# Running the scores two steps ahead in a fused ViT layer, with the side work placed anew

## The chip, the cores and the metric

The kernel runs on one core of a Trainium2 chip. The metric is the device time of one execution in microseconds (us); the median of three runs of the kernel before is 2177.81 us (2173.88 to 2178.31).

## The reference

The kernel computes one layer of a vision transformer tower for 64 images of 3x224x224 (float32):

```python
h = patches(x) @ W.T + b                       # 196 tokens of 768 -> 192
qkv = layernorm(h, g, b) @ qkv_w.T + qkv_b     # 12 heads of 16
attn = q @ k.T * 16 ** -0.5                    # 196 x 196
attn = attn - 0.2 * (3x3 neighbours of attn, the centre left out)
h = h + softmax(attn) @ v
# expert layer: router (192 -> 192 -> 8), the best 2 of 8 experts, each 192 -> 768 -> 192
h = h + sum_e w_e * (relu(layernorm(h) @ W1_e.T + b1_e) @ W2_e.T + b2_e)
```

## The kernel before

There are two phases. The attention phase (here changed) takes some 1230 us and the expert phase the rest; the second starts when the first has stored all rows and is not touched.

The attention phase works on 32 pairs of images. A pair has six **steps**: three groups of four heads for the first image, then for the second. Each engine runs its own in-order program, and what is in the loop body is written out by hand as a software pipeline: at step `kk` an engine works on parts of several steps and pairs. `Step(body, kk, ahead)` is the step that lies `ahead` steps further, `Pair(body, kk, ahead)` the pair that lies `ahead` pairs further, and `k = kk % 6` is the step within the pair, called step 0 to step 5 below. A loop body has two pairs; in its second the kernel also prepares a part of the experts' weights ("pack").

In each step:

- TensorE computes `scores` of four heads (L607, s_bank, two banks that alternate by head), of the step **one** ahead. VectorE takes their row maxima (`row_maxima`, L824) and splits them into two float16 parts (`split_maxima`, L832, L835).
- TensorE transposes these parts (`transpose_max`, L647) and ScalarE copies them into eight extra rows of q_stack (`copy_max_rows`, L1037), so that `scores_less_max` (L623, t_bank, again two banks) gives the scores, transposed and with the maximum taken off, in one matmul. This is for the same step that the maxima came from, so all of it lies between a step's scores and the next step's `scores_less_max`.
- ScalarE takes the exponentials (L1020), TensorE multiplies by v (`mix`, L636) for the step before, ScalarE copies this out (L1027), TensorE transposes it back (L589), and VectorE divides by the sums (`normalise`, L847, L851) for two steps before.

The neighbour sum is folded into q and k: `beside` (GpSimd, L1201) and `tilde` (VectorE, L912) add a token's neighbours. Plain and tilde forms are split into float16 high (ScalarE, L1073, L1082) and low parts (VectorE, L921, L931), stored to memory by two DMAs (`store_parts`) and read back by six (`stack`, L384), which lay three 32-row blocks for q and three for k over all 12 heads into q_stack and k_stack (double buffered by pair). The first scores of a pair wait for all six.

The **side work**, spread over a pair's six steps, prepares later pairs: cast and split of the patches for pair +2 (`high_patches`, ScalarE L1001; `split_patches`, GpSimd L1193), their projection (`project_patches`, four blocks of 18 matmuls, L519 to L521), `take_h`, layer norm statistics and layer norm (GpSimd), transposition, `project_qk`, `take_qk`, `project_v`, `take_v`. The second layer norm ("_n") of finished pairs runs in step 1 to 4 of the pair after: `sum_rows`, `statistics_n`, `inverse_deviation_n`, `layernorm_n`, `high_rows`, `low_rows`. All DMAs of this phase are issued in order by SyncE's queue, which waits at each for its own condition. Its program at step 3 of the first body also blanks some memory (`blank_memory`).

## Time and profile before

| | |
|---|---|
| median of three runs | 2177.81 us |
| the profiled execution: time, span | 2189.16 us, 2187.4 us |
| TensorE busy (share of the span) | 1891.2 us (86%) |
| VectorE busy | 1461.1 us (67%) |
| ScalarE busy | 1266.8 us (58%) |
| GpSimd busy | 1152.0 us (53%) |
| attention phase: last transposition of attention output ends at | some 1222 us |
| mean granted TensorE clock | 0.925 of full speed |

The busy times overlap, since the engines run beside each other. A matmul's recorded length includes its way through the array, so that TensorE can start another before it ends. The clock is a share of 2.4 GHz; 0.50 is 1.2 GHz. Engine names in rows: PE is TensorE, PEld its weight loads, DVE VectorE, ACT ScalarE, POOL GpSimd, SP SyncE (SPq its queue of DMAs).

### The profile page before, as it was taken

Reading aid. Unit: us, or ns where it says so; the run is one execution under the profiler, and the core shown is the slowest. Engines: PE = TensorE matmul, PEld = TensorE weight load, DVE = VectorE, ACT = ScalarE, POOL = GpSimd, SP = SyncE. Lnnn points to the kernel's source line nnn. Section 1 sums busy time; section 2 is a strip of 40 time slices with the busy share of each in tenths; the row PEclk is TensorE's granted clock in tenths of the full one; section 3 lists DMA queues with packets and bytes.
Section 4 is the critical chain, followed back from the end, with each engine's and each line's share of the span. In section 5 each row is a group of like instructions: output and inputs, shape, how many; then the busy total and the mean of one; then the engine's idle time right before and its main releaser. Section 6 shows DMA issues by size and latency. Waiting matters only on the chain. (4 is left out here: it accounts for less than half of the span.)

```text
span 2187.4 us, 54001 instructions
## 1 busy us (share of the span) xinstructions
PE 1891.2 (86%) x17949; PEld 1406.2 (64%) x17949; DVE 1461.1 (67%) x4652; ACT 1266.8 (58%) x2469; POOL 1152.0 (53%) x1069
## 2 busy tenths in 40 slices
PE   4758888888888989898888479999999999999991
PEld 3546666666666666666665256777777777777771
DVE  4658888888888888888887345655555555554440
ACT  3557788787878788787877323433434343333330
POOL 3335555555555545555552254666666666654452
PEclk7878999999999999999999559999999999999996
DMA  4564746666574747575664237787877878798876
GB/s 142 144 187 143 202 147 190 168 182 168 173 197 146 215 142 198 161 195 157 183 173 132 65 106 197 186 211 184 206 185 205 190 201 194 190 195 184 180 176 193
DMA packets 356572, 382.56 MB, mean 175 GB/s; under 512 B 138388, under 2 KB 319952, under 8 KB 352144
## 3 DMA queue, kind: packets, MB, share of 16 engines
q1 hardware_dynamic: 314768, 338.64, 55.3%
q0 software_dynamic: 41664, 42.12, 11.1%
q8 instruction: 80, 1.31, 0.2%
q14 instruction: 60, 0.49, 0.1%
HBM read 232.83 MB, written 135.46 MB: 168 GB/s over the span
## 5 line engine op out<-in xcount | busy, mean ns | idle before, releaser
L1838 ACT ACTIVATE mh<-mid_bank 128x512 bf16<-128x512 f32 x336 | 200.8, 598 | 464.0 <-PE mid_bank L1529 349.6
L824 DVE TENSOR_REDUCE row_max<-s_bank 98x2 f32<-98x392 f32 x768 | 396.6, 558 | 97.6 <-PE s_bank L607 94.7
L1750 DVE SCALAR_TENSOR_TENSOR ml<-mid_bank,mh 128x512 bf16<-128x512 f32 x336 | 231.6, 689 | 341.9 <-ACT mh L1838 333.7
L1020 ACT ACTIVATE probs<-t_bank 98x392 f32<-98x392 f32 x768 | 340.6, 498 | 42.1 <-PE t_bank L623 31.1
L1904 POOL DMA_INDIRECT sums<-y_out,tail x168 | 265.1, 1578 | 172.9 <-DVE y_out L1780 95.8
L1543 PE MATMUL y_bank<-wst,mh 128*128 128x192 bf16 x1344 | 330.0, 246 | 8.3 <-DVE y_out L1780 7.5
L1546 PE MATMUL y_bank<-wst,ml 128*128 128x192 bf16 x1344 | 330.1, 246 | 0.0
L1545 PE MATMUL y_bank<-wst,mh 128*128 128x192 bf16 x1344 | 329.8, 245 | 0.0
L623 PE MATMUL t_bank<-q_stack,k_stack 104*98 104x196 f16 x1536 | 248.6, 269 | 40.0 <-ACT probs L1020 25.5
L1193 POOL TENSOR_TENSOR x_lo<-x_buf,x_hi 128x588 f16<-128x588 f32 x128 | 188.7, 1478 | 170.6 <-ACT x_hi L1001 112.8
L1889 POOL DMA_INDIRECT slots<-row_r,spot x196 | 190.7, 973 | 98.0 <-issue 56.7
L623 PEld LDWEIGHTS t_bank<-q_stack,k_stack 104*98 104x98 f16 x1536 | 152.5, 130 | 112.3 <-ACT probs L1020 108.6
L519 PE MATMUL p_bank<-wtok_h,x_hi 128*98 128x192 f16 x768 | 201.7, 263 | 18.2 <-POOL x_lo L1193 18.2
L607 PE MATMUL s_bank<-k_stack,q_stack 96*98 96x196 f16 x1536 | 204.0, 256 | 6.1 <-DVE row_max L824 5.3
L520 PE MATMUL p_bank<-wtok_l,x_hi 128*98 128x192 f16 x768 | 199.7, 260 | 0.0
L521 PE MATMUL p_bank<-wtok_h,x_lo 128*98 128x192 f16 x768 | 198.7, 259 | 0.0
L1037 ACT COPY q_stack<-m_bank 8x784 f16<-8x784 f16 x192 | 154.4, 804 | 66.5 <-PE m_bank L647 63.5
L636 PE MATMUL o_bank<-probs,v_buf 98*32 98x196 f32 x3072 | 171.5, 341 | 18.1 <-ACT probs L1020 18.0
L1201 POOL TENSOR_TENSOR beside<-padded 128x1176 f32<-128x1176 f32 x32 | 68.7, 2146 | 195.3 <-ACT padded L1064 195.3
L607 PEld LDWEIGHTS s_bank<-k_stack,q_stack 96*98 96x98 f16 x1536 | 153.2, 130 | 12.7 <-DVE row_max L824 7.4
L1543 PEld LDWEIGHTS y_bank<-wst,mh 128*128 128x128 bf16 x1344 | 134.3, 100 | 41.1 <-issue 19.5
L1545 PEld LDWEIGHTS y_bank<-wst,mh 128*128 128x128 bf16 x1344 | 131.0, 97 | 19.6
(236 smaller groups left out, 4515.7 us busy)
## 6 DMA issues: line engine op xcount, KB each, us to landing
wst<-packed SPq DMA_DIRECT2D x56, 1584.0 KB
x_buf<-in_x_t SPq DMA_DIRECT2D x32, 1176.0 KB, 9.0
q_stack<-stack_parts SPq DMA_DIRECT2D x96, 294.0 KB, 4.8
k_stack<-stack_parts SPq DMA_DIRECT2D x96, 294.0 KB, 6.7
stack_parts<-qk_hi SPq DMA_DIRECT2D x32, 588.0 KB, 2.9
stack_parts<-qk_lo SPq DMA_DIRECT2D x32, 588.0 KB, 2.8
sums<-h_buf SPq DMA_DIRECT2D x32, 294.0 KB
h_in<-sums SPq DMA_DIRECT2D x32, 294.0 KB
```

The costliest lines, as they stand in the source:

```text
L519: nc.tensor.matmul(out, x_hi[:, f, tokens], wtok_h[:, f, :], start=(f == 0), stop=False)
L520: nc.tensor.matmul(out, x_hi[:, f, tokens], wtok_l[:, f, :], start=False, stop=False)
L607: last = nc.tensor.matmul(s_bank[hh % 2][0:HALF, u, 0:TOKENS], q_stack[st.q][0:PARTS, head, head_cols(st, u)], k_stack[st.q][0:PARTS, head ...
L623: last = nc.tensor.matmul(out, k_stack[st.q][:, head, head_cols(st, v)], q_stack[st.q][:, head, head_cols(st)], start=True, stop=True)
L824: nc.vector.reduce_max(row_max[st.odd][:, :, hh:hh + 1], s_bank[hh % 2][0:HALF, :, 0:TOKENS], AX.X).then_inc(max_ready, 1)
L1020: nc.scalar.activation(probs[st.odd][:, hh], t_bank[hh % 2][0:HALF, :, 0:TOKENS], ACT.Exp).then_inc(probs_ready, 1)
L1543: nc.tensor.matmul(o, mh[n % MID][:, cols], high, start=(c == 0 and j % 2 == 0), stop=False, skip_group_check=True)
L1545: nc.tensor.matmul(o, mh[n % MID][:, cols], low, start=False, stop=False, skip_group_check=True)
L1546: last = nc.tensor.matmul(o, ml[n % MID][:, cols], high, start=False, stop=False, skip_group_check=True)
L1750: nc.vector.scalar_tensor_tensor(ml[n % MID][:], mid_bank[n % MID_PS][:], 0.0, mh[n % MID][:], ALU.max, ALU.subtract).then_inc(ml_ready, 1)
L1838: nc.scalar.activation(mh[n % MID][:], mid_bank[n % MID_PS][:], ACT.Relu).then_inc(mh_ready, 1)
L1904: nc.gpsimd.indirect_dma_start(out=total_rows, out_offset=bass.IndirectOffsetOnAxis(ap=to, axis=0), in_=y_out[q][:, j, :], in_offset=None, ...
```

## The change

- The scores are computed two steps ahead (`LOOK`), with their maxima and the split of these. `transpose_max` and `copy_max_rows` stay one step ahead, so the split that they use is made a step earlier.
- The stacks are read back by group of heads, 18 DMAs for a pair in place of six, and the scores of a group wait for its own six. The stores and the first two groups move to step 2 (the low store and what follows it), the third to step 3.
- Patches: loads, casts and splits run three pairs ahead (casts in steps 2 to 5, splits in 3, 4, 5 and 0); the projection, still two pairs ahead, runs in steps 0, 1 and 2 in place of 1 and 2. TensorE's side work is divided between a place among the heads (`between_heads`, before the last two heads' `scores_less_max`) and one at the end.
- VectorE: both `take_h` and the statistics are in step 2; `statistics_n` alone in step 3; both `take_v` in step 4; `normalise` comes after the work between the maxima. GpSimd: the layer norm in step 3, `sum_rows` waits for the plain low part, the second layer norm's work is in step 4.
- ScalarE: `layernorm_n` is divided between steps 0 and 1 of the pair after next, `high_rows` is in step 3, `take_high_tilde` is among the exponentials, and `take_qk` comes after `copy_max_rows`.
- The fill interleaves pairs 0 and 1 and loads pair 2; the pipeline begins at step -4 and drains for 12 steps in place of 7.

```diff
 BODY_PAIRS = 2
 BODY_STEPS = BODY_PAIRS * STEPS
 BODIES = PAIRS // BODY_PAIRS
-DRAIN = STEPS + 1
+DRAIN = 2 * STEPS
+LOOK = 2
+FILL = 4

...
@@ -136,13 +138,16 @@
-    step(0, -1)
+    for kk in range(-FILL, 0):
+        step(0, kk)
     for body in range(2):
         for kk in range(BODY_STEPS):
             step(body, kk)
-    with eng.Fori(2, BODIES - 1) as body:
+    with eng.Fori(2, BODIES - 2) as body:
         for kk in range(BODY_STEPS):
             step(body, kk)
+    for kk in range(BODY_STEPS):
+        step(BODIES - 2, kk)
     for kk in range(BODY_STEPS + DRAIN):
         step(BODIES - 1, kk)
...
@@ -374,15 +386,15 @@
-            def stack(pr, low):
                     sp.wait_ge(parts_stored[low], 16 * (pr.u + 1))
                     for which, r in (((0, 0), (0, 2), (1, 0), (1, 1)), ((0, 1), (1, 2)))[low]:
...
+                        sp.dma_start((q_stack, k_stack)[which][pr.q][32 * r:32 * r + 32, HG * g:HG * (g + 1)],
+                                     src[:, :, g]).then_inc((q_stacked, k_stacked)[which][g], 16)

             def rows(dram, pr):
                 return dram[bass.ds(pr.u, 1)].rearrange("o c p e -> p (o c) e")
@@ -456,35 +468,44 @@
                     for low in range(2):
...
+                    for g in range(GROUPS):
+                        for low in range(2):
+                            stack(Pair(0, 0, 0), low, g)
                     store_h(Pair(0, 0, 1))
+                elif kk < 0:
+                    return
                 elif k == 0:
-                    load_x(Pair(body, kk, 2))
+                    load_x(Pair(body, kk, 3))
                     load_h(Pair(body, kk, -1))
-                    store_rows(Pair(body, kk, -2))
                 elif k == 1:
                     if kk == 1 and not (isinstance(body, int) and body == 0):
                         store_part(body - 1)
                     elif kk == BODY_STEPS + 1:
                         store_part(body)
+                    store_parts(Pair(body, kk, 1), 0)
+                elif k == 2:
+                    store_parts(Pair(body, kk, 1), 1)
+                    for g in range(2):
+                        for low in range(2):
+                            stack(Pair(body, kk, 1), low, g)
+                elif k == 3:
                     for low in range(2):
-                        store_parts(Pair(body, kk, 1), low)
-                    for low in range(2):
-                        stack(Pair(body, kk, 1), low)
-                elif k == 3:
+                        stack(Pair(body, kk, 1), low, 2)
                     store_y(Pair(body, kk, -1))
                 elif k == 4:
                     store_h(Pair(body, kk, 2))
+                elif k == 5:
+                    store_rows(Pair(body, kk, -2))
                 if kk == 3 and isinstance(body, int) and body == 0:
                     blank_memory()
...
@@ -597,9 +625,9 @@
-                    if st.first and heads[0] == 0:
-                        pe.wait_ge(q_stacked, (st.pair + 1) * STACKED)
-                        pe.wait_ge(k_stacked, (st.pair + 1) * STACKED)
+                    if st.image == 0 and heads[0] == 0:
+                        pe.wait_ge(q_stacked[st.group], (st.pair + 1) * STACKED)
+                        pe.wait_ge(k_stacked[st.group], (st.pair + 1) * STACKED)
...
-            def before_max(body, kk):
+            def between_heads(body, kk):

                 k = kk % STEPS
-                if k in (1, 2):
-                    project_patches(Pair(body, kk, 2), k - 1, 0)
+                if k == 0:
+                    project_patches(Pair(body, kk, 2), 0, 0)
+                elif k == 1:
+                    project_patches(Pair(body, kk, 2), 0, 1, range(PCH // 2, PCH))
+                elif k == 2:
+                    project_patches(Pair(body, kk, 2), 1, 1)
                 elif k == 3:
                     project_v(Pair(body, kk, 1), 0, (0, 1))
+
+            def after_heads(body, kk):
+
+                k = kk % STEPS
+                if k == 0:
+                    project_patches(Pair(body, kk, 2), 0, 1, range(PCH // 2))
+                elif k == 1:
+                    project_patches(Pair(body, kk, 2), 1, 0)
+                elif k == 3:
+                    project_v(Pair(body, kk, 1), 1, (0, 1))
                 elif k == 4:
-                    project_v(Pair(body, kk, 1), 1, (1,))
                     transpose_xn(Pair(body, kk, 2), 0)
-                elif k == 5:
-                    project_qk(Pair(body, kk, 2), 0)
-                    project_qk(Pair(body, kk, 2), 1)
-
-            def after_max(body, kk):
-
-                k = kk % STEPS
-                if k in (1, 2):
-                    project_patches(Pair(body, kk, 2), k - 1, 1)
-                elif k == 3:
-                    project_v(Pair(body, kk, 1), 1, (0,))
-                elif k == 4:
                     transpose_xn(Pair(body, kk, 2), 1)
                 elif k == 5:
-                    project_qk(Pair(body, kk, 2), 2)
+                    for i in range(BLOCKS):
+                        project_qk(Pair(body, kk, 2), i)
...
-                        for c in range(2):
-                            project_patches(pr, half, c)
-                        project_v(first, 0, (0, 1))
-                        project_v(first, 1, (0, 1))
-                    transpose_xn(pr, 0)
-                    transpose_xn(pr, 1)
-                    for i in range(BLOCKS):
-                        project_qk(pr, i)
+                for half in range(2):
+                    for c in range(2):
+                        project_patches(first, half, c)
+                pe.wait_ge(weights_in, 16 * len(LOADS))
+                pe.wait_ge(consts_set, CONSTS)
+                transpose_xn(first, 0)
+                transpose_xn(first, 1)
+                for c in range(2):
+                    project_patches(second, 0, c)
+                for i in range(BLOCKS):
+                    project_qk(first, i)
+                for c in range(2):
+                    project_patches(second, 1, c)
+                project_v(first, 0, (0, 1))
+                project_v(first, 1, (0, 1))
+                transpose_xn(second, 0)
+                transpose_xn(second, 1)
+                for i in range(BLOCKS):
+                    project_qk(second, i)
...
-                if kk == -1:
+                if kk == -FILL:
                     fill_pipeline()
-                scores(Step(body, kk, 1), (0, 1))
+                scores(Step(body, kk, LOOK), (0, 1))
                 mix(Step(body, kk, -1))
                 transpose_back(Step(body, kk, -2))
                 scores_less_max(Step(body, kk, 0), (0, 1))
-                scores(Step(body, kk, 1), (2, 3))
+                scores(Step(body, kk, LOOK), (2, 3))
+                if kk >= 0:
+                    between_heads(body, kk)
                 scores_less_max(Step(body, kk, 0), (2, 3))
-                if kk >= 0:
-                    before_max(body, kk)
                 transpose_max(Step(body, kk, 1))
                 if kk >= 0:
-                    after_max(body, kk)
+                    after_heads(body, kk)
...
@@ -926,59 +961,61 @@
                 k = kk % STEPS
-                if kk == -1:
+                if kk == -FILL:
                     fill_pipeline()
-                row_maxima(Step(body, kk, 1), (0, 1))
-                normalise(Step(body, kk, -2))
+                row_maxima(Step(body, kk, LOOK), (0, 1))
                 if kk >= 0:
                     if k == 1:
                         take_low_plain(Pair(body, kk, 1))
                     elif k == 2:
                         take_h(Pair(body, kk, 2), 0)
-                    elif k == 3:
-                        statistics(Pair(body, kk, 2), 1)
+                        statistics(Pair(body, kk, 2), 0)
+                    elif k == 4:
+                        take_v(Pair(body, kk, 1), 0)
+                        take_v(Pair(body, kk, 1), 1)
                     elif k == 5:
                         split_low(Pair(body, kk, 2))
-                row_maxima(Step(body, kk, 1), (2, 3))
-                split_maxima(Step(body, kk, 1))
+                normalise(Step(body, kk, -2))
+                row_maxima(Step(body, kk, LOOK), (2, 3))
+                split_maxima(Step(body, kk, LOOK))
                 if kk >= 0:
                     if k == 0:
                         add_tilde(Pair(body, kk, 1))
                     elif k == 1:
                         take_low_tilde(Pair(body, kk, 1))
                     elif k == 2:
-                        statistics(Pair(body, kk, 2), 0)
+                        take_h(Pair(body, kk, 2), 1)
+                        statistics(Pair(body, kk, 2), 1)
+                    elif k == 3:
                         statistics_n(Pair(body, kk, -1))
-                        take_h(Pair(body, kk, 2), 1)
-                    elif k == 3:
-                        take_v(Pair(body, kk, 1), 0)
                     elif k == 4:
-                        take_v(Pair(body, kk, 1), 1)
                         take_xt_a(Pair(body, kk, 2))
...
@@ -1005,6 +1042,9 @@
             act.wait_ge(weights_in, 16 * len(LOADS))

             for i in range(2):
+                if i == 1:
+                    for tile in range(TILES):
+                        high_patches(Pair(0, 0, 1), tile)
                 for hh in range(HG):
                     nc.scalar.copy(k_stack[i][PARTS:STACK, hh::HG, :],
...
@@ -1124,36 +1160,35 @@
-                if kk == -1:
+                if kk == -FILL:
                     fill_pipeline()
                 copy_mixed(Step(body, kk, -1))
                 exponentials(Step(body, kk, 0), (0, 1))
-                if kk >= 0 and k < 2:
-                    high_patches(Pair(body, kk, 2), 2 * k)
+                if k >= 3:
+                    high_patches(Pair(body, kk, 3), k - 2)
+                elif k == 0:
+                    layernorm_n(Pair(body, kk, -2), (0, 1))
+                elif k == 1:
+                    take_high_tilde(Pair(body, kk, 1))
                 exponentials(Step(body, kk, 0), (2, 3))
+                copy_max_rows(Step(body, kk, 1))
+                if k == 2:
+                    high_patches(Pair(body, kk, 3), 0)
                 if kk >= 0:
                     if k == 0:
                         take_high_plain(Pair(body, kk, 1))
                     elif k == 1:
-                        take_high_tilde(Pair(body, kk, 1))
-                    elif k == 5:
-                        take_qk(Pair(body, kk, 2), 0)
-                        take_qk(Pair(body, kk, 2), 1)
-                    if k == 3:
-                        layernorm_n(Pair(body, kk, -1))
-                    elif k == 4:
-                        high_rows(Pair(body, kk, -1))
-                copy_max_rows(Step(body, kk, 1))
-                if kk >= 0:
-                    if k < 2:
-                        high_patches(Pair(body, kk, 2), 2 * k + 1)
+                        layernorm_n(Pair(body, kk, -2), (2, 3))
+                    elif k == 3:
+                        high_rows(Pair(body, kk, -2))
                     elif k == 4:
                         take_xt_b(Pair(body, kk, 2))
                         split_high(Pair(body, kk, 2))
-                    if kk in (8, 10):
-                        high_part(body, kk // 2 - 4)
                     elif k == 5:
-                        take_qk(Pair(body, kk, 2), 2)
+                        for i in range(BLOCKS):
+                            take_qk(Pair(body, kk, 2), i)
+                    if kk in (8, 9):
+                        high_part(body, kk - 8)
...
@@ -1233,34 +1268,39 @@
-                if kk == -1:
-                    first = Pair(0, 0, 0)
+                if kk == -FILL:
+                    first, second = Pair(0, 0, 0), Pair(0, 0, 1)
                     split_patches(first, (0, 1, 2, 3))
+                    split_patches(second, (0, 1))
                     pool.wait_ge(consts_set, CONSTS)
                     inverse_deviation(first)
                     layernorm(first)
+                    split_patches(second, (2, 3))
                     add_beside(first)
-                    split_patches(Pair(0, 0, 1), (0, 1, 2, 3))
-                    inverse_deviation(Pair(0, 0, 1))
-                    layernorm(Pair(0, 0, 1))
+                    inverse_deviation(second)
+                    layernorm(second)
...
-                elif k == 0:
+                if k == 0:
                     add_beside(Pair(body, kk, 1))
                     if Pair(body, kk, 1).there:
                         pool.wait_ge(tilde_ready, Pair(body, kk, 1).u + 1)
-                    split_patches(Pair(body, kk, 2), (0,))
+                    split_patches(Pair(body, kk, 2), (3,))
                 elif k == 1:
-                    split_patches(Pair(body, kk, 2), (1, 2, 3))
+                    if Pair(body, kk, 1).there:
+                        pool.wait_ge(plain_lo_ready, Pair(body, kk, 1).u + 1)
                     sum_rows(Pair(body, kk, -1))
-                elif k == 2:
-                    inverse_deviation_n(Pair(body, kk, -1))
                 elif k == 3:
-                    inverse_deviation(Pair(body, kk, 2))
-                    layernorm(Pair(body, kk, 2))
-                elif k == 4:
-                    low_rows(Pair(body, kk, -1))
+                    split_patches(Pair(body, kk, 3), (0,))
+                    if kk >= 0:
+                        inverse_deviation(Pair(body, kk, 2))
+                        layernorm(Pair(body, kk, 2))
+                elif k > 3:
+                    split_patches(Pair(body, kk, 3), (k - 3,))
+                    if kk >= 0 and k == 4:
+                        inverse_deviation_n(Pair(body, kk, -1))
+                        low_rows(Pair(body, kk, -2))
```

## Rows read from the trace of the kernel before

**Rows 1.** Stretches; after the microseconds each engine's busy time, then PEclk, DMA share, GB/s.

```profile
400.00:800.00 400.00, 354.08 (x3780) 265.61 (x3778) 340.64 (x885) 324.01 (x628) 214.42 (x215) 0.96 0.63 179
```

**Rows 2.** The same view, one row for each of one pair's six steps, 0 to 5.

```profile
594.40:598.40 4.00, 3.35 (x36) 2.17 (x35) 2.90 (x9) 2.91 (x7) 2.15 (x1) 0.95 0.34 124
598.40:607.00 8.60, 6.37 (x74) 5.18 (x75) 7.76 (x11) 7.77 (x13) 4.63 (x3) 1.00 0.13 53
607.00:613.10 6.10, 6.00 (x76) 5.06 (x74) 5.09 (x18) 3.12 (x7) 3.09 (x2) 1.00 0.97 260
613.10:618.20 5.10, 4.44 (x54) 3.30 (x53) 4.92 (x21) 3.48 (x9) 3.31 (x8) 1.00 1.12 199
618.20:622.90 4.70, 4.55 (x52) 3.25 (x51) 3.93 (x10) 4.20 (x9) 3.43 (x5) 1.00 1.10 328
622.90:628.90 6.00, 5.53 (x53) 3.55 (x52) 4.25 (x11) 5.32 (x12) 1.57 (x1) 1.00 0.80 286
```

**Rows 3.** Waits from 400 to 1100 us: who for whom, total, times, longest.

```profile
PEld t_bank L623 <- ACT probs L1020: 71.2, 220, 1.2
PE m_bank L647 <- DVE max_parts L835: 36.1, 51, 1.0
```

**Rows 4.** Timeline of a step 1: start us, us, engine, line, instruction, [idle before it <-releaser].

```profile
605.18 0.17 DVE L835 SCALAR_TENSOR_TENSOR max_parts<-row_max,max_parts 98x8 f16<-98x8 f32 x1
605.41 0.26 PE L647 MATMUL m_bank<-ident,max_parts 98*128 98x98 f16 x2 [1.01 <-DVE max_parts L835]
605.71 0.80 ACT L1037 COPY q_stack<-m_bank 8x784 f16<-8x784 f16 x1 [0.73 <-PE m_bank L647]
```

**Rows 5.** Timeline, ScalarE: the L1073 of step 0, one for each pair.

```profile
128.36 1.17 ACT L1073 CAST qk_hi<-padded 128x1176 f16<-128x1176 f32 x1
598.60 1.19 ACT L1073 CAST qk_hi<-padded 128x1176 f16<-128x1176 f32 x1
632.91 1.20 ACT L1073 CAST qk_hi<-padded 128x1176 f16<-128x1176 f32 x1
1164.91 1.17 ACT L1073 CAST qk_hi<-padded 128x1176 f16<-128x1176 f32 x1
```

**Rows 6.** Timeline, TensorE: first and last of 18 patch matmuls in one step.

```profile
602.72 0.28 PE L519 MATMUL p_bank<-wtok_h,x_hi 128*98 128x192 f16 x1
604.15 0.25 PE L521 MATMUL p_bank<-wtok_h,x_lo 128*98 128x192 f16 x1
```

**Rows 7.** Timeline: two subtractions, with GpSimd idle and with GpSimd reading beside them.

```profile
1167.89 1.37 DVE L921 TENSOR_TENSOR qk_lo<-padded,qk_hi 128x1176 f16<-128x1176 f32 x1
601.73 2.23 DVE L921 TENSOR_TENSOR qk_lo<-padded,qk_hi 128x1176 f16<-128x1176 f32 x1
625.70 0.56 DVE L893 TENSOR_TENSOR x_b<-xt_b,x_b 64x392 bf16<-64x392 f32 x1
659.97 1.27 POOL L1231 TENSOR_TENSOR pack<-stage,pack 128x576 bf16<-128x576 f32 x1 [1.20 <-ACT pack L1108]
660.02 1.65 DVE L893 TENSOR_TENSOR x_b<-xt_b,x_b 64x392 bf16<-64x392 f32 x1
```

**Rows 8.** Timeline of the first body: memory blanking, then the patches of pair 3.

```profile
98.88 8.84 SPq L437 DMA_DIRECT2D slots<-blank  x8
117.90 0.43 SPq L366 DMA_DIRECT2D x_buf<-in_x_t  x1
127.00 0.68 ACT L1001 CAST x_hi<-x_buf 128x588 f16<-128x588 f32 x1 [17.62 <-DMA x_buf<-in_x_t]
```

**Rows 9.** Timeline of the fill: pair 1's normalised rows, then the first maxima.

```profile
57.05 2.18 POOL L1183 TENSOR_TENSOR xn<-centred,rstd 98x512 f32<-98x512 f32 x3 [0.17 <-POOL centred L1177]
69.16 2.07 DVE L824 TENSOR_REDUCE row_max<-s_bank 98x2 f32<-98x392 f32 x4 [4.99 <-PE s_bank L607]
```

**Rows 10.** The stacks' DMAs: two issues, and their row of the DMA table.

```profile
607.94 1.30 SPq L384 DMA_DIRECT2D q_stack<-stack_parts  x2
k_stack<-stack_parts SPq DMA_DIRECT2D x96, 294.0 KB, 6.7
```

106 lines of the change are left out of this document (54 added, 52 removed).

## The prediction

> **What bounds the kernel now.** I read the busy shares first: over the whole span TensorE is busy 86% of the time, but the change touches the attention phase alone, so I read that by itself. From 400 to 800 us TensorE is busy 354.08 of 400 us, VectorE 340.64 and ScalarE 324.01 [rows 1]. None is at its limit, and all three are near it. A pair is best measured by the one instruction that ScalarE runs once for each pair, L1073: from the third to the last there are 29 pairs in 1164.91 - 128.36 = 1036.55 us, so 35.7 us each; the pair that I follow below takes 34.3 [rows 5]. TensorE's idle share (11.5%) makes 4.1 us of a pair.
>
> The waits say what this idle time is [rows 3]. Twenty pairs lie in that stretch. TensorE's transposition of the maxima waits for VectorE's split for 36.1 us, 1.8 us a pair, and its weight loads for t_bank wait for ScalarE's exponentials 71.2 us (3.6 us a pair, much of it beside running matmuls). The timeline of a step 1 shows the first one's form [rows 4]: VectorE's split begins at 605.18, TensorE, idle for 1.01 us, transposes at 605.41, ScalarE, idle for 0.73 us, copies at 605.71, and only then can the next step's `scores_less_max` run. So scores, maxima, split, transposition, copy, next scores form a ring through three engines, and it closes once in each step, whatever the other work.
>
> The view by steps shows how the side work lies in this ring [rows 2]. The longest engine of steps 0 to 5 is busy 3.35, 7.77, 6.00, 4.92, 4.55 and 5.53 us, together 32.1 us; the steps take 4.0, 8.6, 6.1, 5.1, 4.7 and 6.0, together 34.5. So 2.4 us are lost in waits although some engine has room. VectorE has 7.76 us of work in step 1 and 2.90 in step 0; a ring that closes in each step can't even that out.
>
> **The change part by part, in the repeated pair.**
>
> Scores two steps ahead. The split that `transpose_max` needs was finished a step earlier, so the 1.8 us a pair of TensorE's wait go, and ScalarE's wait for the transposition with them. No instruction is added. What is late next: s_bank has two banks as before, so TensorE still can't be more than two heads ahead of the maxima, and `mix` and `scores_less_max` still wait for the exponentials. Each engine may now lag the other by about one half of a step, not by more.
>
> TensorE's side work. 18 patch matmuls take 604.15 - 602.72 + one more, 1.5 us [rows 6]. Four such blocks were in steps 1 and 2, now 1.5 are in step 0, 1.5 in step 1 and one in step 2. Step 0 grows by 2.2 to 5.6 us, step 1 falls by 0.8 to 5.6, step 2 by 1.5 to 4.5; a block of v (0.4) goes from step 4 to 3: 4.8 and 4.2; step 5 stays at 5.5. A block between the heads also covers the time in which the first exponentials run, where `scores_less_max` has waited so far: I take half of the 0.9 us or so of this wait that was not covered.
>
> VectorE. Same instructions. The `tilde` sum (1.4 us) ran late enough to fall into step 1's stretch; it counts to step 0 (4.3). Step 1 is then 6.4, less what follows from the port (below). `statistics_n` (1.6) leaves step 2 for step 3, and in return both halves' `take_h` and statistics lie in step 2, both `take_v` in step 4: some 5.1, 4.3, 4.5 and 4.3 us for steps 2 to 5.
>
> ScalarE. Step 2 held nothing but the fixed work, 3.1 us [rows 2]. To this come, each by what it took: in step 0 half a layer norm (0.95) and L1073 (1.2); in step 1 the other half and the high tilde (1.3); one patch cast (0.68, [rows 8]) in each of steps 2 to 5; in step 3 `high_rows` (0.8), in step 4 1.5, in step 5 three `take_qk` (2.0). That is 5.3, 5.4, 3.8, 4.6, 5.3 and 5.8.
>
> The subtraction and GpSimd. `take_low_plain` (L921) takes 1.37 us where GpSimd is idle and 2.23 where GpSimd subtracts patches beside it [rows 7]. Now three of four patch subtractions leave that place and `sum_rows` waits for this very instruction; the one left starts as `tilde` ends, and the maxima (1.03) run first. I take 0.5 to 0.85 us a pair as gained, and step 1 of VectorE at 5.7. There is a price in the other direction: `split_low` in step 5 has two subtractions with both inputs in SBUF, and GpSimd's `low_rows` and a patch subtraction now lie near it. The row for it is the same instruction L893 with 0.56 us alone and 1.65 us beside GpSimd's 1.27 us [rows 7]. It stands ahead of `project_qk`, so it delays TensorE directly. The bounds are 0 (no meeting) and two such meetings, 2.2 us; I take 0.6, half of one, since GpSimd's 19 us of work are spread over 33 us.
>
> The Trainium skill has a rule for this, in "SBUF — State Buffer", section "Who interferes with whom": a VectorE instruction with two SBUF inputs contends with a GpSimd instruction that reads SBUF, and whichever comes first keeps the port for its whole length. By that rule the 0.85 us are gained in full where they don't meet, and each meeting in step 5 costs up to the whole of GpSimd's instruction. The trace agrees: 1.65 is about 0.56 plus what was left of 1.27.
>
> The stacks. 18 DMAs in place of 6 mean twelve more issues on SyncE's queue. Two issues took 1.30 us [rows 10], for three times the data; I take between 0.35 and 0.65 us each, so 4 to 8 us more of a queue that has some 25 us free in a pair. The first group's six are issued some 4.6 us after the low tilde is ready (store 3 us, then two more issues) and are wanted two steps later, some 10 us. The median landing is 6.7 us for a whole block under load [rows 10], and a third of it should take less: nothing is lost. The added waits (six semaphores for two, at four places) cost between 0 and 0.5 us a pair; before L921, where four waits stood, no gap beyond 0.04 us is seen, so I take 0.1.
>
> Sum of a pair. The longest engine of each step is now 5.6, 5.7, 5.1, 4.8, 5.3 and 5.8, together 32.3. This is hardly less than the 32.1 of before: it is the 2.4 us of waits that go, not work. What remains of waiting I put at 0.1 (semaphores), 0.6 (port), and 0.3 for `project_qk`, whose third block waits for ScalarE's `take_qk` now that this comes after the row copy, less the 0.45 of covered exponentials: 0.5. With half of the pairs carrying 1.3 us of pack work, the size of the pack row [rows 7], I get 32.3 + 0.5 + 0.6 = 33.4; engines that even out over two steps should give back some 0.4: **33.0 us a pair against 35.7**. For 29 pairs that is 78 us. Since the 35.7 hold some stretches at the lower clock early in the phase, which may stay, I take 70.
>
> **The rest of the phase.** In the first body the patches of pair 3 are loaded behind the blanking DMAs: issued at 117.90, in use at 127.00, with ScalarE idle for 17.62 us [rows 8]. With loads three pairs ahead this load comes before the blanking. The next load (pair 4) now stands behind it and is wanted two steps later than pair 3 was, some 12 us. So some 12 of 17.6 us go; bounds 5 and 17.6.
>
> The fill: pair 1's normalised rows come at 59.2 us, and the first maxima at 69.16 [rows 9]. GpSimd now subtracts pair 1's patches ahead of pair 0's neighbour sum, so that pair 1's rows should come some 13 us earlier. One more step goes before the first exponentials, 2 us. I take 11 us, bounds 4 and 15. The last six steps, which have no side work, lose their wait for the split (about 0.5 each): 3 us. The longer drain runs the same chain of the last pair, with nothing beside it: 0, at most 3 us lost.
>
> **Sum.** 70 + 12 + 11 + 3 = 96 us. The profiled execution took 2189.16 us, 11 us over the median of the runs, which I leave as it is: 2189 - 96 = 2093 for a profiled one, and 2177.8 - 96 = **2082 us** for the median.
>
> **Rivals.**
>
> Rival A, the port takes it back. `split_low` meets both `low_rows` and a patch subtraction in each pair, 2.2 us in place of 0.6, straight ahead of `project_qk`. Then a pair takes 34.6, the gain there is 1.1 x 29 = 32, with the rest 58 us: some 2120 us. For it: GpSimd's work in step 4 ends just there. Against: the pow and the small operations between give it gaps. Chance 17%.
>
> Rival B, evening out works fully. VectorE's 0.85 (85%) and the engines' sums say that a pair could take what the busiest engine needs, TensorE's 31.4 us. With 31.8 us a pair the gain is 3.9 x 29 = 113, and 139 with the rest: some 2040 us. For it: all three engines' loads are now alike in all steps. Against: two banks each of s_bank and t_bank. Chance 15%.
>
> Rival C, slower: the stacks come late. The first group is wanted a step earlier than before, and is behind two stores, two dozen issues and SyncE's waits. If its last DMA, issued 4.6 us after the low tilde, lands 9 to 10 us later (the patch load of [rows 8] took 9.1), it is 4 us late in each pair, and TensorE stands in step 4: 29 x 4 = 116 us against the 96 gained, some 2198 us. It decides from a landing of some 9 us on. For it: bursts of the DMA engines in steps 2 to 4 (shares of 0.97 to 1.12, [rows 2]). Against: before, all six blocks landed within the 11 us that step 5 left them, and no wait for them is seen. Chance 6%.
>
> Rival D: the ring was only one of several, and the exponentials' wait takes its place, so that a pair takes 35.3 and only fill and blanking gain: 2177.8 - 12 - 26 = 2140 us. For it: 3.6 us a pair of waits for the exponentials. Against: those are between engines that now have slack in each step. Chance 8%.
>
> **How the numbers follow.** The forecast of 2082 has 54%, with its own range of 2060 to 2110. The range for 8 in 10 takes in rival A and nearly reaches B: 2045 to 2140. 0.2% (4.4 us) is about what a measurement can tell from no change. Faster: 54 + 17 + 15 + 8 less a few for bad luck in D, 91%; same 2%; slower 7%.
>
> **What would show it.** The time between two L1073 falls from 35.7 to 33; the wait of the transposition for the split is gone; L921 takes below 1.9 us; L893 and L892 tell of rival A by their means; no wait of the scores for a stack; the blank stall is under 8 us, first maxima before 60 us. I am wrong if the pair takes over 35 or if TensorE waits for stack DMAs in step 4.

## The result and the profile after

The changed kernel takes 2218.47 us (median of four runs, 2216.93 to 2227.03), the kernel before 2175.85 beside it (2169.55 to 2178.31): a ratio of 1.0208, 95% interval 1.0173 to 1.0244. It is slower by 43 us; the forecast was 2082, and 2045 to 2140 the range. The profiled execution spans 2225.0 us in place of 2187.4. All the loss lies in the attention phase: the expert phase's first matmul comes at 1290.27 us in place of 1242.20, 48.1 later. What follows it, which is untouched, took 935 us in place of 945; why it took less isn't shown.

The busy shares of the stretch of [rows 1] have fallen on every engine, TensorE's from 354.08 to 331.39 us, at nearly the same clock. No engine became the bound; all wait more.

```profile
400.00:800.00 400.00, 331.39 (x3473) 240.49 (x3472) 330.27 (x818) 300.08 (x582) 196.15 (x201) 0.94 0.55 167
```

The timeline of ScalarE's high plain part, once for each pair (now L1113), against [rows 5]:

```profile
107.54 1.17 ACT L1113 CAST qk_hi<-padded 128x1176 f16<-128x1176 f32 x1
157.75 1.17 ACT L1113 CAST qk_hi<-padded 128x1176 f16<-128x1176 f32 x1
198.62 1.17 ACT L1113 CAST qk_hi<-padded 128x1176 f16<-128x1176 f32 x1
1215.17 1.17 ACT L1113 CAST qk_hi<-padded 128x1176 f16<-128x1176 f32 x1
```

These are the third, fourth, fifth and last start. The third is 20.8 us ahead of that before (128.36), the last 50.3 behind (1164.91). In between, at the fifth, 198.62 stands against 206.81: 8.2 ahead. From there 27 pairs lose 58.5 us. Below, "pair time" is always the mean of 24 pairs, from the 7th start to the 31st: 35.41 us before, **37.70 after**, where 33.0 was forecast (from 35.7, which [rows 5] give over a stretch with slower first pairs). Waits "a pair" are over the same 24 pairs, so they differ a little from what the fences of 400 to 1100 us give.

The view of waits of 400 to 1100 us, after, against [rows 3]:

```profile
PEld s_bank L635 <- DVE row_max L859: 42.6, 102, 0.9
PE m_bank L675 <- DVE att L886: 72.1, 37, 3.1
PE t_bank L651 <- ACT probs L1060: 20.1, 31, 1.0
PE s_bank L635 <- DVE row_max L859: 16.1, 37, 0.7
```

The transposition's wait for the split is gone, as forecast. But the same instruction (now L675) now waits for L886, `normalise`, and twice as long: 72.1 us where the old wait had 36.1. No wait for a stack's DMA is listed in this stretch.

A look at VectorE by line (line, output and input, shapes, count, busy us, mean ns), 400 to 1100 us, after:

```profile
L867 DVE TENSOR_SCALAR max_parts<-row_max 98x8 f16<-98x8 f32 x111 | 43.6, 393 | 4.7
L927 DVE TENSOR_TENSOR x_al<-xt_a,x_ah 128x392 bf16<-128x392 f32 x19 | 38.3, 2017 | 11.1 <-ACT x_b L1092 9.8
L928 DVE TENSOR_TENSOR x_b<-xt_b,x_b 64x392 bf16<-64x392 f32 x19 | 29.3, 1541 | 0.6
L956 DVE TENSOR_TENSOR qk_lo<-padded,qk_hi 128x1176 f16<-128x1176 f32 x18 | 24.9, 1384 | 20.8 <-ACT qk_hi L1113 20.8
```

The plain low part (L921 before, now L956) takes 1384 ns in every pair where its mean was 2194. The two subtractions of `split_low` (now L927, L928), 556 to 567 ns where they are alone, take 2017 and 1541; their means before were 567 and 1107. I call **port excess** what VectorE's instructions take beyond their undisturbed times, per pair, over the same 24 pairs (a measure of time, named after the port of the prediction's rule): 1.70 us before (0.82 L921, 0.54 L893, 0.33 the maxima's split), 3.78 after (1.45 L927, 0.98 L928, 1.33 the split, L867).

Both losses in one stretch of the timeline, a step 5, and ahead of it a split of the maxima that is held (start us, duration, engine, line; in brackets the idle time before it and who ended it):

```profile
882.29 1.81 POOL L1243 TENSOR_TENSOR att<-att,h_in 98x768 f32<-98x768 f32 x1 [2.94 <-DVE att L886]
883.12 1.02 DVE L867 TENSOR_SCALAR max_parts<-row_max 98x8 f16<-98x8 f32 x1
...
901.36 1.64 POOL L1261 TENSOR_TENSOR row<-xn_n,row 98x768 f16<-98x768 f32 x1
902.56 2.12 DVE L927 TENSOR_TENSOR x_al<-xt_a,x_ah 128x392 bf16<-128x392 f32 x1 [1.09 <-ACT x_b L1092]
902.95 1.31 POOL L1228 TENSOR_TENSOR x_lo<-x_buf,x_hi 128x588 f16<-128x588 f32 x1
904.22 1.59 POOL L1266 TENSOR_TENSOR pack<-stage,pack 128x576 bf16<-128x576 f32 x1
904.72 1.52 DVE L928 TENSOR_TENSOR x_b<-xt_b,x_b 64x392 bf16<-64x392 f32 x1
906.27 0.21 DVE L882 RECIPROCAL recip<-m_bank 98x8 f32<-98x8 f32 x1
906.51 0.29 DVE L886 TENSOR_TENSOR att<-m_bank,recip 98x128 f32<-98x128 f32 x1
906.95 0.32 PE L675 MATMUL m_bank<-ident,max_parts 98*128 98x98 f16 x2 [3.06 <-DVE att L886]
907.31 0.81 ACT L1077 COPY q_stack<-m_bank 8x784 f16<-8x784 f16 x1 [2.48 <-PE m_bank L675]
```

VectorE's subtraction begins under GpSimd's `row` and ends 0.42 us after the *second* GpSimd instruction, `x_lo` (902.95 + 1.31 = 904.26), though `pack` has begun by then; the next ends 0.43 us after `pack`. Together they take 3.64 us for 1.13 us of work. The normalisation stands behind them, TensorE stands 3.06 us for it, and ScalarE for TensorE.

Why does the transposition of a maximum wait for a normalisation? Both transpositions of a step, the maxima's and `transpose_back`'s, write m_bank. `transpose_max` holds two waits, one for the split and one for VectorE to have read the bank in `normalise` of the same step. In the old order `normalise` ran before the work between the maxima and was long done; the change put it behind that work.

The first pairs, view of waits of 60 to 200 us, after:

```profile
POOL att L1243 <- DMA h_in<-sums: 21.6, 1, 21.6
ACT x_hi L1038 <- DMA x_buf<-in_x_t: 5.0, 1, 5.0
```

ScalarE's wait behind the blanking transfers fell from 17.62 us [rows 8] to 5.0, but GpSimd now waits 21.6 us for an `h_in` load behind the same transfers. That is why the fourth start is only 8.5 us ahead (157.75 against 166.26) where the third had been 20.8.

### The profile page after: what moved, and what is told of

Read it like the earlier page. It is cut to its first block and busy times, and to the rows that moved or that the text cites. A ratio compares the mean times of both kernels' runs of the same rounds, so it can differ in the third digit from the quotient of the medians.

```text
span 2225.0 us, 54385 instructions
## 1 busy us (share of the span) xinstructions
PE 1889.0 (85%) x17949; PEld 1396.1 (63%) x17949; DVE 1496.4 (67%) x4652; ACT 1274.4 (57%) x2469; POOL 1136.7 (51%) x1069
## 5 line engine op out<-in xcount | busy, mean ns | idle before, releaser
L859 DVE TENSOR_REDUCE row_max<-s_bank 98x2 f32<-98x392 f32 x768 | 395.3, 557 | 110.0 <-PE s_bank L635 109.6
L1228 POOL TENSOR_TENSOR x_lo<-x_buf,x_hi 128x588 f16<-128x588 f32 x128 | 172.0, 1346 | 298.2 <-ACT x_hi L1038 234.0
L635 PE MATMUL s_bank<-k_stack,q_stack 96*98 96x196 f16 x1536 | 224.4, 257 | 48.7 <-DVE row_max L859 38.0
L651 PE MATMUL t_bank<-q_stack,k_stack 104*98 104x196 f16 x1536 | 224.2, 258 | 40.2 <-ACT probs L1060 36.5
L635 PEld LDWEIGHTS s_bank<-k_stack,q_stack 96*98 96x98 f16 x1536 | 145.2, 126 | 92.9 <-DVE row_max L859 84.5
L543 PE MATMUL p_bank<-wtok_h,x_hi 128*98 128x192 f16 x768 | 192.8, 251 | 10.6 <-POOL x_lo L1228 10.3
L544 PE MATMUL p_bank<-wtok_l,x_hi 128*98 128x192 f16 x768 | 191.9, 250 | 0.0
L545 PE MATMUL p_bank<-wtok_h,x_lo 128*98 128x192 f16 x768 | 191.9, 250 | 0.0
L1583 PEld LDWEIGHTS y_bank<-wst,mh 128*128 128x128 bf16 x1344 | 134.4, 100 | 24.9 <-issue 5.3
L675 PE MATMUL m_bank<-ident,max_parts 98*128 98x98 f16 x384 | 50.1, 213 | 111.2 <-DVE att L886 109.5
```

The source lines that it names most:

```text
L543: nc.tensor.matmul(out, x_hi[:, f, tokens], wtok_h[:, f, :], start=(f == 0), stop=False)
L544: nc.tensor.matmul(out, x_hi[:, f, tokens], wtok_l[:, f, :], start=False, stop=False)
L635: last = nc.tensor.matmul(s_bank[hh % 2][0:HALF, u, 0:TOKENS], q_stack[st.q][0:PARTS, head, head_cols(st, u)], k_stack[st.q][0:PARTS, head ...
L651: last = nc.tensor.matmul(out, k_stack[st.q][:, head, head_cols(st, v)], q_stack[st.q][:, head, head_cols(st)], start=True, stop=True)
L859: nc.vector.reduce_max(row_max[st.odd][:, :, hh:hh + 1], s_bank[hh % 2][0:HALF, :, 0:TOKENS], AX.X).then_inc(max_ready, 1)
L1583: nc.tensor.matmul(o, mh[n % MID][:, cols], high, start=(c == 0 and j % 2 == 0), stop=False, skip_group_check=True)
```

## The experiments

**Theory.** Two things that the forecast missed or priced too low: the shared m_bank with `normalise` late, and meetings of GpSimd with VectorE at new places. **Rivals:** the lookahead itself costs; or the new placement of TensorE's and ScalarE's side work costs, whatever becomes of these two.

**Each cure alone, then both.** The first puts the normalisation back:

```diff
                 row_maxima(Step(body, kk, LOOK), (0, 1))
+                normalise(Step(body, kk, -2))
...
-                normalise(Step(body, kk, -2))
                 row_maxima(Step(body, kk, LOOK), (2, 3))
```

> The changed kernel with one line moved: normalise stands directly after the first two row maxima again, ahead of the side work of the step. Theory T1 (the late normalise is the loss): the transposition of the maxima may only write its bank once normalise of the same step has read its own half of it, and in the changed kernel TensorE waits 72.1 us for that between 400 and 1100 us, 3.9 us a pair of 37.5. With the line back this wait should nearly go, a pair take 34.0 to 35.0 us in place of 37.5, and the whole some 75 to 100 us less than 2218, so 2115 to 2145. Theory T2 (the port is the loss): VectorE's step 5 still holds split_low with 3.6 us in place of 1.1, so project_qk still waits for it; a pair stays above 36.5 and the whole above 2190. Theory T3 (the lookahead itself costs, by coupling through s_bank): no more than 20 us are gained.

The second makes GpSimd wait in step 4, before `low_rows`, until `split_low` is done:

```diff
                     if kk >= 0 and k == 4:
                         inverse_deviation_n(Pair(body, kk, -1))
+                        if Pair(body, kk, 2).there:
+                            pool.wait_ge(x_split, 4 * (Pair(body, kk, 2).u + 1))
                         low_rows(Pair(body, kk, -2))
```

> The changed kernel with one wait added on GpSimd: low_rows, and all that follows it (the patch split of step 5, the pack work), start only after VectorE's split_low of step 5. T2 (the port): L927 and L928 fall from 1.93 and 1.53 us to some 0.57 each, VectorE's step 5 is 2.3 us shorter, normalise and project_qk come 2.3 us earlier, a pair takes 35.3 and the whole some 2150 (2140 to 2165). T1 alone: the same, since normalise waits behind split_low: the wait of TensorE for normalise in step 5 falls from 3.1 to some 0.8 us. T1 and T2 differ in e1 and agree here. If the delay of GpSimd's patch split holds up the projection of patches (a new wait of TensorE for x_lo), the gain is smaller.

> Both edits: normalise first and GpSimd's wait for split_low. T1: hardly better than the normalise edit alone, since then only project_qk stands behind split_low: 0 to 1 us a pair less. T2: project_qk comes 2.3 us earlier than in e1, so 1.5 to 2.3 us a pair less than e1 and some 60 us less in all. My forecast of 33.0 us a pair held for this state: whole 2080 to 2110.

Measured: ratio 1.0033 (1.0015 to 1.005) and 36.38 us a pair with the first; 0.9943 (0.9925 to 0.996) and 35.60 with the second; 0.9984 (0.9968 to 0.9999) and 36.10 with both. Each takes away a good part of the loss, and they don't add. The first alone comes out near what the second theory expected. Both together are only 0.3 us a pair better than the first alone, where the second theory expected 1.5 to 2.3, and with GpSimd's wait in place, `normalise` first makes the pair 0.5 us longer. The view of waits of the first (400 to 1100 us) says a part of why:

```profile
PE p_bank L580 <- DVE x_b L928: 44.7, 20, 2.4
PE s_bank L635 <- DVE row_max L859: 32.3, 36, 1.4
```

The wait for `normalise` is gone, and the same late subtraction holds `project_qk` (L580) instead, 2.2 us a pair. So the 72.1 us were in large part the meetings, seen through the queue of VectorE. In the second, VectorE by line:

```profile
L867 DVE TENSOR_SCALAR max_parts<-row_max 98x8 f16<-98x8 f32 x118 | 60.2, 510 | 4.9
L927 DVE TENSOR_TENSOR x_al<-xt_a,x_ah 128x392 bf16<-128x392 f32 x19 | 10.8, 567 | 12.0 <-ACT x_b L1092 10.9
L928 DVE TENSOR_TENSOR x_b<-xt_b,x_b 64x392 bf16<-64x392 f32 x19 | 10.7, 564 | 0.6
L840 DVE SCALAR_TENSOR_TENSOR pack<-stage,pack 64x384 f16<-64x384 f32 x10 | 23.0, 2304 | 0.0
```

`split_low` is undisturbed, but GpSimd's delayed work now meets the split of the maxima and `pack` (543 ns alone). The port excess is 3.96 us, no less than the 3.78 of the changed kernel. The meetings moved from in front of `project_qk` to places that hurt less. Over the 24 pairs this version also had more clock, 0.98 granted where the changed kernel has 0.95, so not all of its gain is the place. With both cures the excess is 4.69 and the clock 0.95 again; how the 0.5 us divides between them isn't shown. A wait in front of one GpSimd instruction doesn't free the port; it shifts the whole rest of GpSimd's queue.

**GpSimd fitted between VectorE's two-input instructions.** Here `sum_rows` waits for the low tilde, `low_rows` goes ahead of the patch split in step 4, the patch split of step 5 waits for `split_low`, and GpSimd's pack waits for VectorE's:

```diff
-                        pool.wait_ge(plain_lo_ready, Pair(body, kk, 1).u + 1)
+                        pool.wait_ge(tilde_lo_ready, Pair(body, kk, 1).u + 1)
                     sum_rows(Pair(body, kk, -1))
...
                 elif k > 3:
+                    if kk >= 0 and k == 4:
+                        low_rows(Pair(body, kk, -2))
+                    if kk >= 0 and k == 5 and Pair(body, kk, 2).there:
+                        pool.wait_ge(x_split, 4 * (Pair(body, kk, 2).u + 1))
                     split_patches(Pair(body, kk, 3), (k - 3,))
                     if kk >= 0 and k == 4:
                         inverse_deviation_n(Pair(body, kk, -1))
-                        low_rows(Pair(body, kk, -2))
...
+                    pool.wait_ge(part_ready, 3 * body + 2)
                     low_part(body)
```

Once with `normalise` first, once late as in the changed kernel:

> The changed kernel with normalise first and GpSimd's work put between VectorE's two-input operations: sum_rows waits for the low tilde in place of the low plain part, low_rows comes before the patch split of step 4, the patch split of step 5 waits for split_low, the pack subtraction for VectorE's. So far the port took 3.7 us a pair in the changed kernel and still 4.7 with normalise first and the one wait for split_low, since other operations met then (the split of the maxima, the pack part). T2 (the port is the loss): these excesses fall from 4.7 to under 2 us, a pair takes 34.5 or less in place of 36.1, ratio to before 0.96 to 0.975. If the port's excess falls but the pair doesn't, it isn't the port.

> The same placing of GpSimd's work with normalise late, as the changed kernel has it. T1: the transposition of the maxima still waits for normalise in step 5, some 1 us a pair, so 0.3 to 1 us a pair slower than with normalise first: ratio 0.965 to 0.985. T2: the same as with normalise first within 5 us.

Measured: with `normalise` first 2120.47 us against 2176.42, ratio **0.9735** (0.9722 to 0.9748), 34.15 us a pair, port excess 1.91. With it late 0.9904 (0.9891 to 0.9918), 35.69 us a pair, the same excess of 1.91, and TensorE waits 1.3 us a pair for `normalise` (expected: 0.3 to 1 us slower than with it first). Now the two causes have each a price of their own. The place of `normalise`: 35.69 - 34.15 = 1.54 us a pair with GpSimd placed anew, 37.70 - 36.38 = 1.32 with the meetings. GpSimd's places: 37.70 - 35.69 = 2.01 with `normalise` late, 36.38 - 34.15 = 2.23 with it first. Together 3.55. The prices are of whole pairs, clock included: with `normalise` late TensorE's busy time is 0.7 to 0.8 us a pair longer for the same work (31.25 against 30.59 us with the meetings, 31.84 against 31.01 without), at 0.95 and 0.93 granted against 0.96 and 0.95. All other parts of the change are in the version with `normalise` first, and it beats the kernel before: the rival that TensorE's and ScalarE's side work is placed badly falls as the cause of the loss. What that placement costs or gives by itself no run shows. I call this the **settled version**. Its waits and VectorE's lines, 400 to 1100 us:

```profile
PE s_bank L635 <- DVE row_max L859: 33.7, 62, 1.2
PE t_bank L651 <- ACT probs L1060: 14.9, 33, 0.9
```

```profile
L870 DVE SCALAR_TENSOR_TENSOR max_parts<-row_max,max_parts 98x8 f16<-98x8 f32 x124 | 42.7, 344 | 4.2
L867 DVE TENSOR_SCALAR max_parts<-row_max 98x8 f16<-98x8 f32 x123 | 38.7, 314 | 5.1
L927 DVE TENSOR_TENSOR x_al<-xt_a,x_ah 128x392 bf16<-128x392 f32 x21 | 11.7, 556 | 0.0
L928 DVE TENSOR_TENSOR x_b<-xt_b,x_b 64x392 bf16<-64x392 f32 x20 | 11.3, 565 | 0.6
```

Neither the transposition's wait nor a long subtraction is left. The split of the maxima is not free yet: 314 ns in the mean for an instruction that takes 171 alone, and its second half, L870, 344. They now meet `low_rows` (L1261) and the patch splits (L1228) of steps 4 and 5, which makes up the 1.91:

```profile
618.81 1.65 POOL L1261 TENSOR_TENSOR row<-xn_n,row 98x768 f16<-98x768 f32 x1
619.84 0.66 DVE L867 TENSOR_SCALAR max_parts<-row_max 98x8 f16<-98x8 f32 x1
620.41 1.33 POOL L1228 TENSOR_TENSOR x_lo<-x_buf,x_hi 128x588 f16<-128x588 f32 x1
620.53 1.24 DVE L870 SCALAR_TENSOR_TENSOR max_parts<-row_max,max_parts 98x8 f16<-98x8 f32 x1
```

**The meeting put into the old kernel.** `low_rows` is moved from step 4 to step 5, to begin as `split_low` does, with the wait that this needs:

```diff
-                elif k == 4:
+                elif k == 5 and kk >= 0:
+                    if Pair(body, kk, 2).there:
+                        pool.wait_ge(x_high, 2 * Pair(body, kk, 2).u + 1)
                     low_rows(Pair(body, kk, -1))
```

> The kernel before with one edit: low_rows of GpSimd runs in step 5, from when ScalarE has written x_ah, and so against VectorE's split_low (in the kernel before it runs in step 4 and meets nothing). T2 (a meeting ahead of project_qk costs its own length): x_al takes 1.5 to 2 us in place of 0.57, a pair 1.0 to 1.5 us more, the whole 30 to 45 us more, ratio 1.014 to 1.02. If the step had room, less than 10 us.

Measured: ratio 1.0287 (1.0273 to 1.0301), 37.54 us a pair, +2.13, more than was expected. The timeline of a pair with pack work, where GpSimd has two instructions in a row:

```profile
610.23 1.64 POOL L1226 TENSOR_TENSOR row<-xn_n,row 98x768 f16<-98x768 f32 x1 [3.03 <-ACT x_ah L1050]
610.59 2.94 DVE L892 TENSOR_TENSOR x_al<-xt_a,x_ah 128x392 bf16<-128x392 f32 x1
611.82 1.28 POOL L1231 TENSOR_TENSOR pack<-stage,pack 128x576 bf16<-128x576 f32 x1
613.56 0.56 DVE L893 TENSOR_TENSOR x_b<-xt_b,x_b 64x392 bf16<-64x392 f32 x1
...
614.18 0.51 PE L554 MATMUL p_bank<-x_ah,wqk_ah 128*128 128x392 bf16 x1 [1.69 <-DVE x_b L893]
```

One instruction of 1.64 us, moved, costs the whole kernel 2.9%. VectorE's subtraction takes 2.94 us here and TensorE stands for 1.69; in the pairs without pack work it takes 1.71. The 2.94 are the 2.51 us that GpSimd had left of its two instructions (to 613.10) and 0.43. Over the 24 pairs the port excess rises by 1.2 us, to 2.86, and TensorE's wait for `split_low` by 1.15, from 0.20 to 1.35. That isn't all of the 2.13: TensorE is also busy 32.56 us a pair in place of 31.22 for the same work, at a granted clock of 0.92 in place of 0.96, and how far the lower clock comes from the longer waits isn't shown.

The Trainium skill's rule ("SBUF — State Buffer", section "Who interferes with whom") that the later instruction waits for the port until the earlier one ends agrees with the pairs without pack work. In those with it the subtraction was under way before GpSimd's second instruction and still waited for that too, which the rule doesn't give; the measurement decides.

**The lookahead without the rest.** In the old kernel, scores two steps ahead, alone, and then with the stacks loaded by group in step 1:

```diff
-                scores(Step(body, kk, 1), (0, 1))
+                scores(Step(body, kk, 2), (0, 1))
...
-                row_maxima(Step(body, kk, 1), (2, 3))
-                split_maxima(Step(body, kk, 1))
+                row_maxima(Step(body, kk, 2), (2, 3))
+                split_maxima(Step(body, kk, 2))
```

> The kernel before with one part of the change alone: scores, maxima and their split run two steps ahead; all side work stays where it was, and the stacks are still read back by six DMAs. T1: the ring was real, so a pair loses the 1.8 us of TensorE's wait for the split and part of ScalarE's for the transposition: 33.9 in place of 35.7, whole 2115 to 2130. T3 (the lookahead costs): a pair takes 35.7 or more, whole at or above 2176. A rival inside T1: the first scores of a pair now stand in step 4 and wait for the stacks' last DMA, which landed near the end of step 3: then a wait of the scores for a DMA of 0.5 to 3 us a pair is seen, and the gain is smaller by it.

> The kernel before with the lookahead of two steps and the stacks read back by group, all 18 DMAs in step 1; all side work as before. The lookahead alone gave ratio 1.028 with 2.3 us a pair of waiting for the stacks' DMA. That wait should go wholly (the first group lands some 4 us earlier). T4: then a pair takes 35.1, about what it took before (ratio 0.99 to 1.00). T1: 33.9 us a pair, ratio 0.975 to 0.98.

Measured: alone 1.0283 (1.0264 to 1.0301), 37.44 us a pair. One wait says why, 2.3 us a pair, and that the loading by group is a condition of the lookahead:

```profile
PE s_bank L610 <- DMA k_stack<-stack_parts: 43.6, 19, 3.0
```

With the stacks by group 0.9952 (0.9938 to 0.9967), 35.03 us a pair; so the lookahead itself doesn't cost, which was the first rival. But 0.4 is gained where the forecast's main term was 1.8 and more. Its waits:

```profile
PE m_bank L594 <- issue: 34.2, 40, 1.1
PE t_bank L628 <- ACT probs L1025: 16.9, 27, 1.0
PE o_bank L641 <- ACT probs L1025: 13.9, 20, 2.0
```

the first of these in the kernel before (L589 there), in the same stretch:

```profile
PE m_bank L589 <- issue: 14.3, 20, 0.9
```

and its place in the timeline of the version by group:

```profile
701.32 0.25 PE L652 MATMUL m_bank<-ident,max_parts 98*128 98x98 f16 x2
...
704.33 0.80 ACT L1042 COPY q_stack<-m_bank 8x784 f16<-8x784 f16 x1
...
705.24 0.64 PE L594 MATMUL m_bank<-ident,mixed 128*98 128x128 f32 x2 [1.07 <-issue]
```

The wait for the split is gone (1.85 us a pair before), and TensorE's next user of m_bank, `transpose_back` (L594), stands for 1.71 us a pair where it had 0.71, until ScalarE has copied the rows out at 705.13; that copy stands behind ScalarE's side work. Another 0.68 are a new wait of `mix` (L641) for the exponentials. So the bank takes back 1.0 of the 1.85 and the exponentials 0.7. The profile puts L594's wait down to "issue", which hides that it is the same bank again: the kernel has it wait for `max_rows_ready`, which that copy signals.

**The new order without the lookahead.** LOOK = 1 in the changed kernel, in the second version above, and in the one with the port and `normalise` settled:

```diff
-LOOK = 2
+LOOK = 1
```

> The changed kernel with LOOK = 1: scores, maxima and split one step ahead again, everything else as changed. Theory T4 (two banks): TensorE can't issue scores more than two heads ahead of the maxima, so the wait for the split only turns into a wait for the bank, and two steps of lookahead give at most 0.5 us a pair; then this kernel takes as long as the changed one within 20 us, and its wait for the split comes back while the wait of the scores for the maxima (52.8 us of both kinds between 400 and 1100 us) shrinks. Theory T1' (the ring was real, its gain is only covered by other losses): this kernel is 1.8 us a pair slower than the changed one, 50 to 60 us more.

> The changed kernel with GpSimd's wait for split_low (as in the run before with that name) and LOOK = 1. T4: within 15 us of the same kernel with LOOK = 2 (ratio to before 0.994), since normalise, the banks and the side work set the pace. T1': 1.5 us a pair slower, ratio to before about 1.015.

> The gates-first version with the scores one step ahead again (LOOK = 1). Theory L1: the order of the change needs the lookahead whatever the port does (5 us a pair were lost without it when the meetings stood): pair time 36.5 us or more, ratio above 1.03. Theory L2: the lookahead only covered the delays of the meetings and of the late normalise; with both gone the pair loses under 0.5 us: pair 34.2 to 34.6, ratio 0.975 to 0.985.

Measured: 1.0848, 1.0837 and 1.0625 (1.0595 to 1.0655), with 42.63, 42.71 and 40.71 us a pair. TensorE waits for the split 6.6 us a pair in the last, over its 24 pairs:

```profile
PE m_bank L675 <- DVE max_parts L870: 115.1, 78, 3.1
PE t_bank L651 <- ACT probs L1060: 8.8, 16, 0.9
```

The expectation that the lookahead only covered the delays of the port falls, and with it that of the two earlier runs, by which the two score banks leave it next to nothing to give: without it the new order loses 6.6 us a pair (an unknown part of it by the clock, 0.83 granted in place of 0.95 from 400 to 1100 us). The new order without the lookahead is 5.3 us a pair worse than the old one, the lookahead in the old order is worth 0.4, both together 1.3. The two are one change: the order puts long side work between a step's scores and its split, and only the lookahead allows that.

**What is left: the two score banks.** Half of each maximum's columns (98 of 196) are left out, first in the second version, then in the settled one:

```diff
-s_bank[hh % 2][0:HALF, :, 0:TOKENS]
+s_bank[hh % 2][0:HALF, :, 0:HALF]
```

> The kernel with GpSimd's wait for split_low, LOOK = 2, and each row maximum taken over the first 98 of 196 columns alone (this leaves out half of that work). If VectorE and the two score banks set the pace (T4), a maximum of some 0.31 us in place of 0.56 takes 5 to 6 us of VectorE's work from a pair, the wait of the scores for the maxima goes, and a pair takes 32 to 33 us in place of 35.7: whole some 90 us less, ratio to before 0.95. If TensorE and ScalarE set the pace, a pair falls by less than 1 us.

> The gates-first version with each maximum taken over 98 of the 196 columns (half of the maxima's work is left out). Theory B: what stands between 34.15 us and the forecast 33.0 is the wait of the scores for a bank, which the maxima free: that wait (1.67 us a pair) goes and the pair takes 33.0 us or less, ratio 0.957 or less. Rival: another chain (ScalarE's exponentials) takes its place and the pair gains under 0.5 us, ratio above 0.967.

Measured: 0.9786 (34.65 us a pair) and 0.9493 (0.9459 to 0.9528), 32.37 us a pair. The wait of the scores for a bank, 1.67 us a pair in the settled version, is 0.17, and TensorE's longest waits (400 to 1100 us) are for the exponentials:

```profile
PE t_bank L651 <- ACT probs L1060: 28.7, 39, 1.2
PE o_bank L664 <- ACT probs L1060: 10.8, 27, 0.8
```

So the settled version is partly held by VectorE's maxima; 1.78 us a pair hang on them. That they do so by freeing the two score banks is what the wait says, but the run doesn't prove it: it also takes 3.9 us a pair of work out of VectorE's queue, and no version has more banks. The forecast's sum of longest engines has no term for this wait.

**The blanking transfers.** Issued one expert at a time over the steps of the first two bodies in place of all at once, in the old kernel with the lookahead by group, and in the settled version:

```diff
+                if kk in (3, 5, 7, 9, 11) and isinstance(body, int) and body == 0:
+                    blank_slots((kk - 3) // 2)
+                if kk in (1, 3, 5) and isinstance(body, int) and body == 1:
+                    blank_slots(5 + kk // 2)
+                if kk == 7 and isinstance(body, int) and body == 1:
+                    blank_packed()
```

> The kernel before with the lookahead of two steps, stacks by group, and the blanking DMAs spread over steps 3, 5, 7, 9, 11 of the first body and 1, 3, 5, 7 of the second, one at a time. The stall of some 17 us for the patches of pair 3 behind them should go, in all kernels so far it only moved from one load to another: 12 to 17 us less than the run without it (ratio 0.9952), so ratio 0.987 to 0.990.

> The gates-first version, with the blanking transfers spread over the steps of the first pairs. Theory: the stall of the first pairs goes, as when the same was done to the lookahead-by-group version (13 us there): pair time unchanged at 34.1 us, ratio to before about 0.968. Rival: the new order is short of nothing at that place and the gain is under 3 us, ratio 0.973.

Measured: 0.9896 (0.9881 to 0.9911) where it was 0.9952, and **0.9674** (0.9644 to 0.9703), 2123.19 us against 2193.07, where it was 0.9735; pair times unchanged (34.99 and 34.14). The fifth start moves from 190.58 to 177.21 us. That is the fastest version with the whole computation, 3.3% ahead of the kernel before and, by the two ratios (0.9674 / 1.0208), 5.2% ahead of the changed one.

## Why the prediction was wrong

- **The waits that go.** The 1.8 us a pair of the split did go. The step "What is late next" named s_bank and the exponentials and passed over m_bank, which three engines share. Moving `normalise` behind the side work was never priced: 1.3 to 1.5 us a pair. And the ring's gain was taken for the lookahead's own: in the old order the lookahead gives 0.4 us, since 1.0 us of the wait pass to the bank's next user and 0.7 to the exponentials. That is near rival D, which had 35.3 us a pair (35.03 here) and named the exponentials alone.
- **The price of the port**, 0.6 with bounds 0 and 2.2, is the mis-sized term: the excess of L927 and L928 rose by 1.89 us a pair (0.54 to 2.43), and that of the split of the maxima by 1.00, which I had not counted since it is so small. In the settled placement the whole excess falls from 3.78 to 1.91, and by the pair times of the versions that differ in GpSimd's places alone this is worth 2.0 to 2.2 us. Rival A had the mechanism, and with 2.2 us its price. Its 34.6 us a pair are 3.1 below the measured 37.70: 1.54 for the place of `normalise`, 1.15 that the sum lacked besides (below), and 2.01 for GpSimd's places where the rival added 1.6. The argument for 0.6, GpSimd's 19 us spread over 33, took meetings as chance; in a written order they fall the same way in each loop body. Before, L893 takes 1.65 and 0.56 us in turn; after, 1.52 and 1.56.
- **L921** gained its 0.8 us as forecast.
- **The sum of a pair** took the longest engine of each step, 32.3, and 0.5 of waits. With the two defects cured, 34.15 is left where 33.0 was forecast, with the score banks' wait of 1.67 in it. "TensorE still can't be more than two heads ahead of the maxima" was written, and costed at nothing.
- **The stacks**: right. Landing 2.5 us, issues mostly 0.43 to 0.47 us each, and no wait but one of 1.3 us in the first pairs; rival C is dead. The issues of a repeated pair come to 8.5 us in place of 3.8, 4.7 more. The forecast's lower bound of 4 left out that the first six get shorter too, but nothing hung on it.
- **The fill and the blanking.** The first maxima came at 60.01 us (forecast: under 60, from 69.16), and the third start 20.8 us earlier, near 11 + 12. Then the same transfers held `h_in`, where the forecast named only the patches of pair 4 as what would now stand behind them. At the fifth start 8.2 of the 23 us were left.
- **The drain**: from the last start to the expert phase 75.1 us in place of 77.3, 2.2 gained, 3 forecast.

In all: forecast -96. Measured in the profile: -8 in the first five pairs, +58.5 in the repeated ones, -2 in the drain.

## What to carry to other kernels

Before an instruction is moved on an in-order engine, list who waits for *it*, and through which shared buffer: a wait removed from a ring can pass to the bank's next user. Place GpSimd's work one by one against VectorE's instructions with two inputs in SBUF and against its `tensor_scalar` on SBUF, the tiny ones too, and check each against its undisturbed time: a meeting comes back in every loop body, and a wait that is added against it can move it to another instruction. When a transfer is moved from behind a burst, see what takes its place in the queue.
